# A four-layer block on one Trainium2 core: the memory and expert stage with four steps of lookahead, a filling written out by hand, and down products by inner unit

## What is computed

```python
# memory (L1_attn), on xn = layernorm(x)
Bm = xn @ W_B + b_B;  Cm = xn @ W_C + b_C
dt = softplus((xn @ W_dt1 + b_dt1) @ W_dt2 + b_dt2)
phi = cumsum(omega_base * dt, axis=1)
content = Bm * xn
real = cumsum(content * cos(phi), axis=1);  imag = cumsum(content * sin(phi), axis=1)
x = x + (Cm * (real * cos(phi) + imag * sin(phi))) @ W_out + b_out + D * xn
# experts (L1_ffn), on xt = layernorm(x)
scores = softmax(xt @ gate_w.T)          # 16 experts in 4 groups
# keep the best 2 groups, in them the best 4 experts; c[t, e] = score or 0
a = silu(xt @ w1[e]) * (xt @ w3[e])      # inner width 64
x = x + sum_e c[:, e] * (a @ w2[e]) + (silu(xt @ ws1) * (xt @ ws3)) @ ws2
```

## Time and profile before

| what | value |
|---|---|
| three runs | 1530.39, 1526.48, 1529.39 us; median 1529.39 us |
| profiled execution | span 1530.5 us, 23116 instructions; the profile states no other time for it |
| PE busy | 1318.1 us, 86% |
| DVE busy | 1026.1 us, 67% |
| ACT busy | 796.0 us, 52% |
| POOL busy | 536.5 us, 35% |
| the stage | from 673.2 to 1037.9 us of the span, of which 101.6 us before the first up product |

### The profile page before, as it was taken

The page is one execution under the profiler, slowest core; times in us unless marked ns, Lnnn a source line. Parts: engine busy times, 40 slices in busy tenths (PEclk is TensorE's granted clock), DMA queues, the critical chain, the costliest instruction groups (busy, mean ns, idle before and its releaser), DMA issues. The chain is left out here.

```text
span 1530.5 us, 23116 instructions
## 1 busy us (share of the span) xinstructions
PE 1318.1 (86%) x7350; PEld 782.0 (51%) x7350; DVE 1026.1 (67%) x2781; ACT 796.0 (52%) x1595; POOL 536.5 (35%) x678
## 2 busy tenths in 40 slices
PE   5899999999997877953579999988899988989898
PEld 1223333333332677941335566557676756877633
DVE  7778888888882675645887786423567563666586
ACT  2467777777775203536546554322445452466554
POOL 3442443342210005439546434431112122443046
PEclk7799999999999888985689999999999999999999
DMA  5211111111101702210033323221132131100001
GB/s 152 61 33 42 54 48 34 50 51 43 43 23 50 185 1 55 64 39 24 14 91 72 62 57 56 57 56 40 60 102 75 60 115 56 35 1 1 1 21 35
DMA packets 80779, 81.23 MB, mean 53 GB/s; under 512 B 19899, under 2 KB 64139, under 8 KB 80659
## 3 DMA queue, kind: packets, MB, share of 16 engines
q1 hardware_dynamic: 77327, 74.06, 18.0%
q0 software_dynamic: 2304, 4.72, 1.4%
q10 hardware_dynamic: 1028, 0.98, 0.2%
HBM read 64.32 MB, written 13.92 MB: 51 GB/s over the span
## 5 line engine op out<-in xcount | busy, mean ns | idle before, releaser
L939 DVE TENSOR_REDUCE a_nm<-a_aps 128x1 f32<-128x512 f32 x512 | 333.7, 686 | 76.8 <-PE a_aps L704 76.7
L903 ACT ACTIVATE a_prob<-a_sps 128x512 f32<-128x512 f32 x512 | 271.5, 597 | 116.3 <-PE a_sps L716 115.3
L704 PE MATMUL a_aps<-a_K,a_Q 96*128 96x512 bf16 x512 | 195.9, 403 | 13.1 <-DMA a_K<-k_parts 12.7
L716 PE MATMUL a_sps<-a_Q,a_K 99*128 99x512 bf16 x512 | 156.9, 386 | 1.2 <-ACT a_prob L903 1.2
L1399 POOL TENSOR_TENSOR p_h<-p_sl,p_t 128x512 f32<-128x512 f32 x72 | 106.5, 1494 | 140.9 <-ACT p_sl L1542 86.5
L725 PE MATMUL a_ops<-a_prob,a_Vg 128*32 128x512 f32 x1024 | 137.2, 610 | 0.0
L704 PEld LDWEIGHTS a_aps<-a_K,a_Q 96*128 96x128 bf16 x512 | 50.4, 98 | 141.4 <-DVE a_nm L939 90.5
L1542 ACT ACTIVATE p_sl<-p_up_a 128x512 f32<-128x512 f32 x72 | 42.9, 597 | 109.1 <-PE p_up_b L1427 109.1
L413 POOL CAST a_ms<-a_mr 16x128 bf16<-16x128 f32 x32 | 9.0, 280 | 245.2 <-ACT a_mr L861 245.1
L1937 POOL TENSOR_TENSOR c_h<-c_h,c_G 128x512 f32<-128x512 f32 x24 | 34.1, 1427 | 171.7 <-DMA c_G<-choice_rows 112.9
L716 PEld LDWEIGHTS a_sps<-a_Q,a_K 99*128 99x128 bf16 x512 | 50.1, 99 | 61.5 <-ACT a_prob L903 30.5
(11 more groups left out here) (585 smaller groups left out, 2794.2 us busy)
## 6 DMA issues: line engine op xcount, KB each, us to landing
p_G<-gates_by_expert SPq DMA_DIRECT2D x32, 512.0 KB, 10.6
c_G<-choice_rows SPq DMA_DIRECT2D x32, 512.0 KB, 6.5
a_Q<-q_parts SPq DMA_DIRECT2D x192, 32.0 KB
a_K<-k_parts SPq DMA_DIRECT2D x31, 96.0 KB
q_parts<-a_partsq SPq DMA_DIRECT2D x7, 384.0 KB, 2.8
k_parts<-a_partsk SPq DMA_DIRECT2D x7, 384.0 KB, 2.8
token_outputs<-m0e_y SPq DMA_DIRECT2D x40, 64.0 KB, 1.5
m0w_w<-in_L_ffn_W SPq DMA_DIRECT2D x1, 2048.0 KB, 8.9
```

What stands on the lines that cost most here:

```text
L704: nc.tensor.matmul(aps[n % 3][:, :], Q[0:MAX, head, q * P:(q + 1) * P], K[0:MAX, head, :], start=True, stop=True).then_inc(a_ready, 1)
L716: nc.tensor.matmul(sps[(NS * u + k) % 3][:, :], K[0:KB, head, k % TC * P:(k % TC + 1) * P], Q[0:KB, head, :], start=True, stop=True).then_ ...
L903: nc.scalar.activation(prob[u % 2][:, k // TC, k % TC, :], sps[n % 3][:, :], ACT.Exp).then_inc(p_done, 1)
L939: nc.vector.tensor_reduce(nm[u % 2][:, s:s + 1], aps[n % 3][:, :], AX.X, ALU.max, negate=True).then_inc(a_used, 1)
```

## The change

The same arithmetic in another order. The loop over `steps` is gone on all engines. A filling of one-off calls comes first, with chunk 0 ahead of all; then steps s = 0 to 7 in which the preparation runs on chunks s+2 to s+4. Five buffers `back` instead of eight, two of `ph`.

```diff
-        steps = range(-8, B + 1)
+        spreads = lambda c: (c + 1) // 2
+        BY_POOL = (1, 2)
...
             def fetch_back(c):
+                wait(pool, x_added, c - NB + 1)
...
+            def turn_content(c):
+                pool.wait_ge(content_made, BY_POOL.index(c) + 1)
+                nc.gpsimd.tensor_tensor(cs[:, :], content[:, :], sn[c % 2][:, :], ALU.mult).then_inc(cs_made, 1)
...
-            def down(c, k):
-                if k == 0:
-                    pe.wait_ge(h_done, NW * (c + 1))
+            def down(c, j):
+                if j == 0:
                     wait(pe, y_added, c)
-                for j in range(NW):
+                pe.wait_ge(h_done, NW * c + j + 1)
+                for k in range(TC):
...
+            def choose_pair(j):
...
+                wait(pe, G0_done, j)
+                nc.tensor.matmul(whole_yps, of_pair[:, j, :], gT[0][:, :], start=True, stop=True).then_inc(chosen, 1)
...
+            def middle(s):
+                pe.wait_ge(a_done, NW * (s + 1))
+                if here(s + 2):
+                    outer(s + 2)
+                if here(s + 3):
+                    turn_first(s + 3)
+                pe.wait_ge(t_done, NW * (s + 1))
+                if here(s + 3):
+                    steps_of_time(s + 3)
+                    input_gates(s + 3)
+                for j in range(NW):
+                    down(s, j)
+                    if j == 1 and here(s + 2):
+                        turn_second(s + 2, up_a[1])
+                    if j == 3 and here(s + 2):
+                        logits(s + 2, up_b[1])
```

ACT's middle holds the same calls, with three table loads and a preload of Silu; `trig(s + 2)` moves between the Silus (its table stays). `keep_pair(j)` is ACT's copy of a one-hot product (of_pair, a matrix of 16 rows with ones for the two experts of a pair, by chunk 0's transposed gates) into G. It stands for chunk 0 in place of the round through DRAM. DVE:

```diff
+            def middle(s):
+                if here(s + 4):
+                    add_back(s + 4)
+                if here(s + 2):
+                    add_memory(s + 2)
+                    second_rstd(s + 2)
+                if here(s + 4):
+                    first_rstd(s + 4)
+                if here(s - 1):
+                    measure_output(s - 1)
+                if here(s + 2):
+                    shift_logits(s + 2, up_b[1])
+                    choose_groups(s + 2)
+                if here(s + 3):
+                    phase_sum(s + 3)
...
+            for s in range(1, B):
                 for j in range(NW):
+                    product(s, j)
+                    if j == 0 and here(s + 2):
+                        phase_rest(s + 2)
+                    if j == 1:
+                        if here(s + 1):
+                            choose_experts(s + 1)
                         add_output(s - 1)
+                    if here(s + 2):
+                        if j == 2:
+                            take_content(s + 2)
...
+                        if j == 7:
+                            read_memory(s + 2)
+                middle(s)
```

More of the change, by code:

```diff
@@ new lines, in _ @@
+            join_tables()
+            turn_first(0)
+            steps_of_time(0)
+            input_gates(0)
+            turn_first(1)
+            steps_of_time(1)
+            outer(0)
+            turn_first(2)
+            steps_of_time(2)
+            input_gates(1)
+            turn_second(0, up_a[1])
+            logits(0, up_b[1])
+            up(0, 0)
+            up(0, 1)
+            turn_gates(0, whole_yps)
+            choose_pair(0)
+            for j in range(2, NW):
+                choose_pair(j - 1)
+                up(0, j)
+                if j == 3:
+                    outer(1)
+                    input_gates(2)
+                if j == 4:
+                    turn_second(1, ops)
+                if j == 5:
+                    logits(1, ops)
@@ L1536, in _ @@
+            turn_gates(1, ops)
+            middle(0)
+            for s in range(1, B):
+                for j in range(NW):
+                    up(s, j)
+                    if here(s + 1) and j == MID:
+                        turn_gates(s + 1, ops)
+                middle(s)
         @block.scalar
@@ new lines, in _ @@
+            first_root(0)
+            copy_first(0)
+            softplus_parts(0)
+            first_root(1)
+            softplus_exp(0)
+            softplus_log(0)
+            copy_first(1)
+            softplus_parts(1)
+            softplus_exp(1)
+            softplus_log(1)
+            nc.scalar.preload_act_table(ACT.Silu)
+            trig(0)
+            nc.scalar.preload_act_table(ACT.Sqrt)
+            first_root(2)
+            copy_first(2)
+            second_root(0)
+            nc.scalar.preload_act_table(ACT.Exp)
@@ L1641, in _ @@
+            keep_gates(1, ops)
+            middle(0)
+            for s in range(1, B):
+                for j in range(NW):
+                    silu(s, j)
+                    if here(s + 2) and j == 2:
+                        trig(s + 2)
+                    if here(s + 1) and j == MID:
+                        keep_gates(s + 1, ops)
+                middle(s)
         @block.vector
@@ L1684, in phase, with take_content, turn_content @@
-            def phase(c):
+            def take_content(c):
+                v.wait_ge(bc_ready, c + 1)
+                v.wait_ge(trig_done, c + 1)
+                last = stt(content[:, :], bps[:, :], bB[:, :], net.xT[:, c * S:(c + 1) * S], ALU.add, ALU.mult)
+                if c in BY_POOL:
+                    last.then_inc(content_made, 1)
+                v.drain()
+            def turn_content(c):
+                tt(cc[:, :], content[:, :], cn[c % 2][:, :], ALU.mult)
+                if c not in BY_POOL:
+                    tt(cs[:, :], content[:, :], sn[c % 2][:, :], ALU.mult)
+                v.drain()
@@ L1720, in add_back @@
                 xt = net.x[:, TC * c:TC * (c + 1), :]
[L1721 removed]
+                tt(xt, xt, back[c % NB][:, :, :], ALU.add).then_inc(x_added, 1)
                 v.wait_ge(x_added, c + 1)
@@ L1787, in _ @@
             v.drain()
[L1788 to L1815 removed]
+            phase_sum(0)
```

422 lines of the change are left out of this document (253 added, 169 removed).

## The result

The changed kernel takes **1556.96 us** (median of 4 runs, 1551.06 to 1561.10), beside 1528.37 for the kernel before: a ratio of 1.0178, 95% interval 1.0154 to 1.0201. It is slower, as forecast, but by 28.6 us where 7.8 were forecast, and outside the range of 1514 to 1553. The profiled execution spans 1557.3 us against 1530.5. Ahead of the stage and behind it the two traces agree within 0.1 us together, so the stage holds the difference: from its first instruction on any engine to the end of its last down it takes 389.5 us and not 362.6.

What follows compares the result with a forecast made beforehand. PE was taken to bound the steps and the chain preparing a chunk the filling. Filling -22.5, steps +25.3 and clock +5 gave +7.8 us on 1529.4: 1537 us, range 1514 to 1553.

Steps and rivals of the forecast that it cites:

- The filling up to the first up: Stage start to first up product: chunk 0 goes first, so the first up starts near 725 instead of 774.8.
- Step 0: Behind the first up: DVE's list 32.5 us plus waits 15.5, r of chunk 2 near 778, step 1 at 794.5.
- DVE's waits for PE: In step 0: 4.5 us of DVE waiting for PE, partly at 1.2 GHz with eight one-hot products added.
- my worse bound: Filling to the start of step 1: -22.5 us forecast, with bounds -28 and -15; the worse is -15.
- The list in the steps: Steps 1 to 5: DVE's list, not PE's 16 us, ends the ups; r ready at 24.2 us.
- the holds: Steps with preparation: POOL's h product delays DVE at five places by 0.95, 4.8 us, bounds 1.2 and 6.
- Rival 1: Steps 1 to 5: DVE's list fits nearly under the ups, a step is 36.4 us; 1518 us, chance 0.31.
- The clock in the steps: Five steps: PE idles 4 us ahead of the outer product; clock falls cost 1 us each, +5, bounds 0 and +14.
- Steps 6 and 7: Last two steps: downs needn't wait 2.39 us for POOL's last h, so 24.5 us each, 49.0 together.
- Rival 3: Whole stage: clock falls in every step and filling at its worse bound, +24, 1554 us; chance 0.13.
- The signs of being wrong: Forecast is wrong if steps 1 to 5 average under 38.5 us, or step 1 starts before 789.
- The scalar operations: DVE in the phase: by the skill's rule these also wait for POOL; without that a step is about 0.9 us shorter.

Runs made afterwards that it cites:

- e6: The changed kernel with five matmuls whose results nobody reads, around chunk 0's gates in step 0: 1565.17 us, 1.019 of the kernel before, one run.
- e11: The changed kernel with unread matmuls in step 0 (five), steps 1 to 5 (four each) and before step 5's second transposes (three): 1.0077 of the kernel before.
- e5: The changed kernel with POOL's h product over only 64 of 512 columns from step 2 on: 1.008 of the kernel before, one run.
- e1: The changed kernel with four matmuls whose results nobody reads ahead of the outer product in steps 1 to 5: 1.0118 of the kernel before.
- e12: The kernel before with downs by inner unit, some moved earlier, and sines of step 0 and later taken behind Silu's table load: 1498.58 us, 0.9801.

## Why the prediction was wrong, by its own steps

- **The filling up to the first up** was right, mechanism and size: the first up at 724.8 where 725 was forecast, the waypoints within 2.2 us, the sine of chunk 0 (ready at 706.7 for 704.5) the worst.
- **Step 0 failed, in one term, DVE's waits for PE.** Of the 15.5 us of waits, the copied gate (3.6 for 3.5), the sines (3.0 for 3) and POOL (about 4.6 for 4.5) came as forecast. The waits for PE were 9.1 us and not 4.5: the prediction had that PE "at this load runs partly at 1.2 GHz", and it did so for all one-hot, up and outer products from 733.6 to 749.9 us, the first two waits, 6.1 us, among them. With PE kept busy these two fell to 1.9 us (e6) and 1.3 (e11), but later waits grew, and all four came to 6.1 and 8.2. So it is the low clock that the term had too small, by the trace; that filling shortens step 0 is not shown. r of chunk 2 was 6.6 us late, 4.6 of them from this term and 0.9 from gates that came at 730.9, step 1 started at 801.3 and not at 794.5, and the filling gained 15.7 us instead of 22.5, about my worse bound. The middle of step 0 was 16.5, as forecast.
- **The list in the steps** was right. r was ready, and the outer product started, 24.3 to 24.8 us into steps 1 to 5, where 24.2 was put; the holds were 4.6 us for 4.8, and e5 showed that they are POOL's. Rival 1 fell with that.
- **The clock in the steps failed.** "Step 2 puts the price of a fall at 2.8; I take 1 each, +5, bounds 0 and +14." The idle time ahead of the outer product was forecast (4 us; 3.6 came), and its price was in the row quoted, but a third of it was put into the sum, with no other reason than that gaps of 2.3 us had left the clock up in step 1 before. It cost 4.4, 1.7, 4.4, 1.7 and some 1.4 us: 13.6, on average 2.7 a step, which is step 2's 2.8 before, and in all next to the upper bound of 14. e1's steps 1 to 4 were 8.3 us shorter than the changed kernel's, of the 12.2 that the falls cost there, and 4.0 shorter than the same unfilled steps in e6; with its matmuls the outer product also started some 0.6 us later in each step.
- **Steps 6 and 7**: 50.9 for 49.0. The gap went from 2.39 to 0.83, but not to nothing (PE waits for the last silu), and step 6 has the four gate transposes and a gap of 0.92.
- **The sum.** 6.8 for the filling, 8.6 for the clock, 1.8 for r in five steps, 1.9 in the last two: 19.1 us, which is all of the stage's miss (26.9 for 7.8), where the medians of the runs missed by 20. Rival 3, "The clock falls in every step and the filling is at its worse bound", is what happened, and its 1554 missed only the small terms; its other reason, that the copied gates go no faster than the round through DRAM, did not come, since the copied gate cost the forecast 3.6 us. It was given 0.13, and the range ended at 1553, just below it. Both halves of rival 3 are the low clock behind a PE that waits more, and so not two mishaps that have to come together; that is how I read the error in the chances.
- **The signs of being wrong** looked to one side only: steps 1 to 5 averaged 42.1 us, not under 38.5, and step 1 started at 801.3, not before 789. Neither sign came, and the forecast was wrong all the same.
- **The scalar operations** of DVE: the trace now has what was missing, that one is held by POOL too. The four of chunk 1's normalisation took 4.26 us beside POOL's operations, the four of chunk 0 1.47 with POOL issuing gathers. This agrees with the Trainium skill's rule (GPSIMD Engine Reference, Specifications), by which VectorE instructions in a 2-port mode or with two SBUF inputs contend with GpSimd; whether these ran in that mode no run shows. In the steps the phase's scalar operations fell outside POOL's products (0.42 and 0.43 us), so the 0.9 us didn't come.

## What to carry to other kernels

A shorter lookahead buys a shorter filling once and pays for it in every step, if it puts two stages of one chunk in series that used to belong to different chunks: follow the circle of waits through one step, not the busy shares (here 36 and 32 of 44 us). Idle time of PE, like the 3.6 us here, should be priced with the low clock behind it, at the whole of what a slow stretch in the trace costs, and the engines that wait for PE pay it as well. Where the clock falls differs from trace to trace of the same code, so one trace doesn't price a fall to better than some us. And signs of being wrong belong on both sides of a forecast. Last, of a change with several parts, the small one may be the good one: downs by inner unit were worth 0.3 per cent alone and 1.4 once they were put where PE stood idle.

## What the runs showed of the hardware

- A DVE operation with two SBUF inputs that starts while POOL's 512-column product runs waits for nearly the whole rest of it: 1.75 us instead of 0.68, 0.81 with a 64-column product. This held for multiplications, a scaled addition (1.60 for 0.69), a scan (1.65 for 1.22), a tiny 128x64 product (1.34 for 0.23) and, beside other POOL operations, for tensor-scalar ones.
- PE's granted clock fell behind idle stretches of 2.0 to 3.7 us in these traces, but not behind each of them: in the changed kernel it fell behind 2.50 us among the ups of step 2 and not behind 2.59 in step 1. The fall moved between traces of the same code, and filling one gap sometimes moved it to the next one (step 5 of e1).
- Sine runs from the table that is loaded for Silu: no load stands between them, and in e12 one load of 1.28 us less took PE's wait for a silu in step 2 from 1.67 to 0.24 us.
